# A graph network with an expert layer on one core: packed, gathered rows for 23 of the 49 aggregation tiles

## What is computed

```python
deg = segment_sum(ones, rows, n) + 1.0          # rows is src, cols is dst
dinv = rsqrt(deg)[:, None]
h = x @ W_in + b_in
for l in range(4):
    h_scaled = h * dinv
    msg = segment_sum(h_scaled[cols], rows, n) * dinv
    global_ctx = mean(h, axis=0) @ Wg[l] + bg[l]
    z = relu((h + msg) @ Wl[l] + bl[l] + global_ctx)
    h = (z - mean(z)) * rsqrt(var(z) + eps) * gamma[l] + beta[l]
```

## Time and profile before

| | |
|---|---|
| Median of 3 runs | 3345.32 us (3343.95 to 3345.57) |
| The profiled execution's span | 3340.5 us |
| TensorE, VectorE, ScalarE, GpSimd busy | 94%, 60%, 25%, 2% of the span |
| Setup, to about 45 us | 45 us |
| Counting, 45 to 597 us | 552 us |
| Flag, scales, table, 597 to 636 us | 39 us |
| Layers 1 to 4 | 573.6, 564.0, 563.4 and 614.0 us |
| Routing and experts, from 2951 us | 389.5 us |

### The profile page before, as it was taken

The page is one execution under the profiler, slowest core; times in us unless marked ns, Lnnn a source line. Parts: engine busy times, 40 slices in busy tenths (PEclk is TensorE's granted clock), DMA queues, the critical chain, the costliest instruction groups (busy, mean ns, idle before and its releaser), DMA issues.

```text
span 3340.5 us, 56169 instructions
## 1 busy us (share of the span) xinstructions
PE 3129.2 (94%) x17421; PEld 1810.2 (54%) x17421; DVE 1989.9 (60%) x5304; ACT 850.9 (25%) x1934; POOL 70.6 (2%) x168
## 2 busy tenths in 40 slices
PE   6888898699999999999999999999999999979998
PEld 4666676344444444444444444444444444458887
DVE  7999999755455445545554555455555555545554
ACT  3777787411111111111111111111111111123222
POOL 0000000000000000000000000000000000000100
PEclk8999999799999999999999999999999999989999
DMA  4222212412222222221222222221222222110000
GB/s 133 79 79 79 71 49 79 115 68 75 69 67 70 74 68 67 68 76 67 67 76 69 67 67 73 72 67 67 77 78 69 76 78 74 62 34 19 17 17 19
DMA packets 134136, 225.44 MB, mean 67 GB/s; under 512 B 12277, under 2 KB 106596, under 8 KB 134018
## 3 DMA queue, kind: packets, MB, share of 16 engines
q1 hardware_dynamic: 131666, 217.53, 20.2%
q0 software_dynamic: 2352, 6.40, 0.7%
HBM read 178.17 MB, written 45.74 MB: 67 GB/s over the span
## 4 chain that ended last, share of the span: by engine, by line
PE 80%; DVE 11%; issue 4%; ACT 2%; DVEq 1%; DMA 1%; SPq 0%; ACTq 0%; POOL 0%; POOLq 0%
PE bank L1342 50%; PE bank L1212 9%; PE bank L1416 5%; PE bank L1422 5%; PE bank L1300 4%; PE bank L1230 2%; PE bank L1198 2%; PE bank L1290 2%; PE bank L1228 1%; PE bank L1236 1%; DMA tab<-in_x 1%; DVE region L865 1%; DVE region L858 1%; DVE st L870 1%; DVE region L878 1%
## 5 line engine op out<-in xcount | busy, mean ns | idle before, releaser
L1342 PE MATMUL bank<-tab,region 128*128 128x512 f16 x9604 | 2143.0, 379 | 11.4 <-DMA region<-adjacency 11.2
L1342 PEld LDWEIGHTS bank<-tab,region 128*128 128x128 fp8e4 x9604 | 940.3, 98 | 1063.0 <-DVE tab L790 17.1
L1212 PE MATMUL bank<-region 128*128 128x320 bf16 x1862 | 316.4, 320 | 49.8 <-DVE region L670 48.3
L670 DVE TENSOR_SCALAR region<-iota_w,src_col,src_w 128x640 bf16<-128x640 int16 x931 | 361.0, 437 | 0.0
L865 DVE SCALAR_TENSOR_TENSOR region<-bank,c_back,bias 128x256 f32<-128x256 f32 x196 | 94.8, 483 | 405.7 <-PE bank L1300 405.7
L1029 ACT ACTIVATE tab<-region 128x640 fp8e4<-128x640 uint8 x490 | 307.2, 712 | 18.5 <-DVE region L701 18.5
L1212 PEld LDWEIGHTS bank<-region 128*128 128x128 f16 x1862 | 232.6, 144 | 124.4 <-DVE region L670 95.7
L1127 ACT ACTIVATE sd<-mv,eps_c 128x1 f32<-128x1 f32 x196 | 57.8, 295 | 820.8 <-DVE mv L872 820.8
L862 DVE TENSOR_TENSOR region<-bank,region 128x256 f16<-128x256 f32 x196 | 83.2, 425 | 297.6 <-ACT region L1125 297.6
L1125 ACT ACTIVATE region<-bank 128x256 f16<-128x256 f32 x196 | 75.3, 384 | 594.9 <-PE bank L1290 594.9
L1416 PE MATMUL bank<-tab 128*128 128x384 f32 (+1 forms) x544 | 177.2, 484 | 2.6 <-DMA b_s<-in_L_ffn_b 2.6
(11 more groups left out here) (194 smaller groups left out, 2143.9 us busy)
## 6 DMA issues: line engine op xcount, KB each, us to landing
region<-adjacency SPq DMA_DIRECT2D x196, 784.0 KB, 4.3
adjacency<-tab SPq DMA_DIRECT2D x12, 3136.0 KB, 13.9
region<-in_x POOLq DMA_DIRECT2D x48, 128.0 KB, 2.3
out<-region SPq DMA_DIRECT2D x48, 128.0 KB, 1.7
tab<-in_x SPq DMA_DIRECT2D x1, 6016.0 KB
tab<-in_L_ffn_W SPq DMA_DIRECT2D x4, 512.0 KB, 4.2
Wg_s<-in_L_gnn_Wg SPq DMA_DIRECT2D x1, 1024.0 KB
region<-in_L_gnn_Wl SPq DMA_DIRECT2D x1, 1024.0 KB, 5.6
```

Source lines behind the costliest of these rows:

```text
L670: ins = v.tensor_scalar(hot_s[:, j, :], iota_w[:], src_col[:, ds(start + j, 1)], src_w[:, ds(start + j, 1)], ALU.is_equal, ALU.mult)
L1212: ins = mm(bank[k % 2 * 2 + half][:, 0:HALF], hot_d[:, :, j], hot_s[:, j, half * HALF:(half + 1) * HALF], start=j == 0, stop=j == WIN - 1)
L1342: ins = mm(acc[a][:, :], A_s[:, a, m, :], tab[:, here + m, :], start=m == 0, stop=m == T - 1)
```

## The change

Of the 49 output tiles 23 are picked, the even ones from 2 to 46. An output tile has about 2041 edges, which reach some 1740 of the 6250 nodes. In layers 2 to 4 a picked tile's aggregation reads only rows that it needs, packed into 17 blocks (CAP) of 128: 17 matmuls stand where 49 stood. The packing keeps a node inside its group of 16 partitions, so each group has 17 x 16 = 272 places (TAKEN).

- **Counting.** VectorE compares each edge's source tile with the 23 picked tiles (two TENSOR_TENSORs a tile, 230 and 207 elements wide); the second matmul of each pair of L1212 gets 23 more columns. ScalarE takes the sign of the counts (23 columns a tile). Before the flag, VectorE sums these and makes a list of candidates (a code for each needed node), TensorE sums the groups, and the flag also turns on if a group has more than 272. SyncE writes the candidates to DRAM and loads them back in another shape, a row for each picked tile and group.
- **Layer 1.** All tiles are aggregated as before. VectorE picks the lists in 2 x 34 rounds of MAX8 and MATCH_REPLACE over 784 columns, three rounds in each of the first 24 tiles (behind L858, behind the split and behind the tile's last operation). ScalarE's queue writes the lists out and loads them back; then GpSimd fetches the picked rows of A by 17 indirect DMAs for each picked tile (from tile 14 and tile 26 on) and writes them out packed. SyncE waits for all of them before it starts any load of layer 2.
- **Layers 2 to 4.** ScalarE's queue writes each finished tile of the table to DRAM as well. At a layer's border GpSimd waits for all 49, then gathers: 17 indirect DMAs of 128 rows of 1 KB for each picked tile, in chunks of 6, 6 and 5, into four slots; a slot is used again once TensorE has read it. TensorE waits for each chunk. The load of A for a picked tile is 272 KB.
- **Order.** In a picked tile the turn and the product of the tile before stand ahead of matmuls 10 and 16, in the full tile behind a picked one ahead of matmuls 22 and 34. VectorE's order is unchanged: `late` is always false, so a tile's whole chain is completed before the sums of the next are taken. The layers' tiles are written out without loops on VectorE and ScalarE, and from layer 2 on on TensorE and SyncE, with constant indices. The reload of x in layer 4 moves from GpSimd's to ScalarE's queue. fgam and fbet are loaded at the end.

The core of the diff:

```diff
+PICKED = list(range(2, T - 2, 2))
+CAP = 17
+TAKEN = CAP * GROUP
+ROUNDS = TAKEN // 8
+PER_STEP = 3
+CHUNK = ((0, 6), (6, 12), (12, CAP))
+SLOTS = 4
+SPARSE_T, SPARSE_MM = 10, 16
+AFTER_T, AFTER_MM = 22, 34
+def late(l, t):
+    return False
...
+                for h in range(2):
+                    sp.wait_ge(pack_out[h], 16 * ((NS + 1 - h) // 2))
+                for l in range(1, LAYERS):
+                    for t in range(T):
+                        a = slot(t)
+                        sp.wait_ge(agg_done, l * T + t + 1)
+                        if picked(t):
+                            sp.dma_start(A32_s[:, a, 0:CAP * P // 4], AspD[PICKED.index(t)]).then_inc(a_in[a], 16)
+                        else:
+                            sp.dma_start(A32_s[:, a, :], A[t].rearrange("p m s -> p (m s)")).then_inc(a_in[a], 16)
...
+            def fetch_pack(q):
+                for j in range(CAP):
+                    nc.gpsimd.indirect_dma_start(pack[q % 2][:, j, :], None, A_rows,
+                                                 bass.IndirectOffsetOnAxis(ap=pick_A[:, q, j:j + 1], axis=0)
+                                                 ).then_inc(pack_in[q % 2], 16)
...
+            c = 0
+            for l in range(1, LAYERS):
+                hold(pool, rows_out[l - 1], 16 * T)
+                for q in range(NS):
+                    for j0, j1 in CHUNK:
+                        if c >= SLOTS:
+                            freed(c - SLOTS)
+                        for j in range(j0, j1):
+                            nc.gpsimd.indirect_dma_start(G[c % SLOTS][:, j - j0, :], None, tab_rows[(l - 1) % 2],
+                                                         bass.IndirectOffsetOnAxis(ap=pick_tab[:, q, j:j + 1], axis=0)
+                                                         ).then_inc(g_in[c % SLOTS], 16)
+                        c += 1
...
+                    v.tensor_tensor(hot_s[:, j0:j1, W:W + NS], pick_id[:, 0:NS].unsqueeze(1).to_broadcast([P, j1 - j0, NS]),
+                                    src_tile[:, ds(start + j0, j1 - j0)].unsqueeze(2).to_broadcast([P, j1 - j0, NS]),
+                                    ALU.is_equal)
...
+            def take(h, r):
+                top = lists[h][0:rows, 8 * r:8 * r + 8]
+                pick_own.done(v.max(top, left[h][0:rows, :]))
+                pick_own.wait()
+                ins = v.match_replace(left[h][0:rows, :], top, left[h][0:rows, :], 0.0)
...
+                for t in range(T):
+                    gathered(l, t)
+                    if l == 0:
+                        picking(t, 0)
+                    split(l, t)
+                    if l == 0:
+                        picking(t, 1)
+                    if not late(l, t):
+                        moments(l, t)
+                        normal(l, t)
+                    if l == 0:
+                        picking(t, 2)
...
+                a.activation(some[:, m, 0:NS], bank[k % 2 * 2 + 1][:, HALF:HALF + NS], ACT.Sign).then_inc(some_set, 1)
...
+                def picked_rows(l, t, c, turn_at, product_at):
+                    n, a, q = l * T + t, slot(t), PICKED.index(t)
+                    for h, (j0, j1) in enumerate(CHUNK):
+                        pe.wait_ge(g_in[(c + h) % SLOTS], 16 * g_count[(c + h) % SLOTS])
+                        for j in range(j0, j1):
+                            if j == turn_at:
+                                turn_u(n - 1)
+                            if j == product_at:
+                                product_u(n - 1, l)
+                            ins = mm(acc[a][:, :], A_s[:, a, j, :], G[(c + h) % SLOTS][:, j - j0, :], start=j == 0,
+                                     stop=j == CAP - 1)
```

More of the change, by code:

```diff
@@ L102, in build @@
     AG = nc.dram_tensor("adjacency_general", [FIELDS * PK, PLANES, P, T, P], BF16).ap()
+    candD = nc.dram_tensor("candidates", [NS, P, T], F32).ap()
+    listD = nc.dram_tensor("lists", [NS * GROUPS, TAKEN], F32).ap()
+    AspD = nc.dram_tensor("packed", [NS, P, CAP * P // 4], I32).ap()
+    TABD = [nc.dram_tensor(f"rows{h}", [P, T, 2 * D], F16).ap() for h in range(2)]
+    A_rows = A.rearrange("t p m s -> (t p m) s")
+    tab_rows = [TABD[h].rearrange("p t f -> (p t) f") for h in range(2)]
     ctx = ExitStack()
@@ L424, in read_flag, with slot @@
             return eng.value_load(flag[0:1, 0:1], min_val=0, max_val=1)
[L426 to L430, removed]
+        def slot(t):
+            return (t - 1) % RING if t else RING
         @block.sync
@@ new lines, in _, with picking, gathered @@
+            SPAN_B = -(-ROUNDS // PER_STEP)
+            def picking(t, part):
+                h, r = t // SPAN_B, t % SPAN_B * PER_STEP + part
+                if h < 2 and r < ROUNDS:
+                    take(h, r)
+                for h in range(2):
+                    if part == 0 and t == (h + 1) * SPAN_B + 2:
+                        chosen_rows(h)
+            def gathered(l, t):
+                n, a, here = l * T + t, slot(t), (l + 1) % 2 * T
+                tile_own.done(v.tensor_tensor(hs, tab[:, here + t, 0:D], tab[:, here + t, D:2 * D], ALU.add))
+                dve.wait_ge(lo_ready, n + 1)
+                tile_own.done(v.tensor_tensor(acc_s, acc[a][:, 0:D], lo_f[:, a, :], ALU.add))
+                tile_own.wait()
+                tile_own.done(v.tensor_scalar(Q, acc_s, c_read[:, t:t + 1], None, ALU.mult))
+                tile_own.wait()
+                v.scalar_tensor_tensor(out=U[:, 0, :], in0=hs, scalar=c_own[:, t:t + 1], in1=Q, op0=ALU.mult,
+                                       op1=ALU.add).then_inc(u_ready, 1)
@@ L844, in one @@
+            for l in range(LAYERS):
                 dve.wait_ge(ctx_done, l + 1)
@@ L909, in one @@
+                if l < LAYERS - 1:
                     dve.wait_ge(tab_ready, (l + 2) * T)
                     dve.sem_inc(hsum_ready, 1)
-            layers(dve, one)
             dve.wait_ge(xsum, T)
@@ L1133, in one @@
-                tiles(act, step, n0)
-            layers(act, one)
+                if l == LAYERS - 1:
+                    for t in range(RING):
+                        again(t)
+                for t in range(T):
+                    take_sums(l, t)
+                    if t and not late(l, t - 1):
+                        rows(l, t - 1)
+                    take_turned(l, t)
+                    if t and late(l, t - 1):
+                        deviation(l, t - 1)
+                        finish(l, t - 1)
+                    if not late(l, t):
+                        deviation(l, t)
+                        if t and late(l, t - 1):
+                            rows(l, t - 1)
+                        finish(l, t)
+                    if l == 0:
+                        for h in range(2):
+                            if t == (h + 1) * SPAN_B:
+                                lists_out(h)
+                            if t == (h + 1) * SPAN_B + 1:
+                                lists_in(h)
@@ L1137, in _ @@
+                rows(l, T - 1)
             act.wait_ge(xmean_done, 1)
@@ L1247, in _ @@
             ins.then_inc(norms_done, 1)
+            pe.wait_ge(taken_set, 1)
+            mm(bank[3][:, 0:NS], same_group, taken, start=True, stop=True).then_inc(taken_sum, 1)
             degrees(T - 1, 2 * MG)
```

373 lines of the change are left out of this document (267 added, 106 removed).

## The result

The changed kernel took 4103.8 us (4087.0 to 4132.7, 4 runs) against 3345.0 us before: a ratio of 1.2279, 95% interval 1.2229 to 1.2329. It is slower by 759 us. The later runs add something that no single comparison shows: **this kernel's time is not the same on every chip.** It took 3550.8 us on chip 5 and 3555.3 us (one execution) on chip 11, but 4162.3 us on chip 12, while the kernel before stayed within 3340 and 3357 us in every comparison. The chip of the first measurement is not on record; it may be chip 12 itself. So two things are to be explained: why the kernel is slower everywhere, and what costs 550 to 610 us more on one kind of chip.

A forecast was written before the change was run, and what follows sets the result against it. VectorE bounds counting, TensorE layers 1 to 3, one tile's serial chain layer 4. 3340.5 - 214 + 15 + 36 + 38 + 5 + 10 = 3230.5 us, forecast 3235 us; range 3185 to 3470 us.

The forecast's parts named there:

- Step 1: Layers 2 to 4: fewer matmuls, limited by the serial chain; 82, 82 and 50 us less, together -214 us.
- rival D: Layer 4: TensorE's clock falls at each of its 46 stalls, some 2 us lost in each, 3317 us; chance 0.05.
- step 6: Before the flag and layer 4: sums and candidates +5 us, row stores nothing, TensorE's clock +10 us (0 to 90).
- Step 2: Layers 2 to 4: GpSimd's gathers take 1.0 us per indirect DMA, hidden but for 7 us a layer at its start.
- rival A: GpSimd's queue: indirect issue takes 1.25 us or more, decides from about 1.16 us on; 3460 us, slower; chance 0.25.
- Step 3: Layer 1: 391 packing DMAs and 23 stores end at 1240 us, delaying layer 2's first load; +15 us.
- Step 4: Layer 1: VectorE's 68 picking rounds of 2.1 us make 24 tiles 13.0 us long against 11.45; +36 us.
- Steps 5 and 6: Counting: two more VectorE comparisons a tile, +38 us; then sums and candidates +5 us, clock in layer 4 +10 us.
- Rival C: GpSimd's issue: VectorE's three TENSOR_SCALARs a tile stop it for 11%, 1.0 becomes 1.11 us; 3278 us; chance 0.15.

The follow-up runs named there:

- experiment 7: Kernel before with GpSimd DMAs that nobody waits for added, another kind (indirect or direct) in each layer: 3342.0 and 3342.6 us against 3342.2 on chip 8.

## Why the prediction was wrong, point by point

- **Step 1, the chain: right in layers 2 and 3, wrong in layer 4.** The kernel without indirect DMAs shows what the step foresaw, TensorE's timeline in layer 2:

```profile
1515.03 0.44 PE L1553 MATMUL bank<-ident,region 128*128 128x128 f32 x2 [0.86 <-DVE region L1036]
...
1523.68 0.44 PE L1553 MATMUL bank<-ident,region 128*128 128x128 f32 x2 [1.29 <-DVE region L1036]
...
1533.62 0.44 PE L1553 MATMUL bank<-ident,region 128*128 128x128 f32 x2 [0.86 <-DVE region L1036]
```

  A pair takes 18.59 us (forecast 19.0), the stalls 0.86 and 1.29 us, ended by VectorE. The two layers gain 100 us each (forecast 82, of which 7 us were taken off for the start of the gathers, which this kernel lacks). In layer 4 the mechanism of **rival D**, given 0.05, is what happened:

```profile
2458.15 0.69 PE L1553 MATMUL bank<-ident,region 128*128 128x128 f32 x2 [2.48 <-DVE region L1036]
2458.64 4.20 PE L1642 MATMUL bank<-tab,region 128*128 128x512 f16 x12
2462.67 0.82 PE L1563 MATMUL bank<-Wx,region 128*128 128x256 f16 x6
...
2471.66 0.61 PE L1553 MATMUL bank<-ident,region 128*128 128x128 f32 x2 [2.78 <-DVE region L1036]
```

  After stalls of 2.5 to 3.2 us the transposes take 0.61 and 0.69 us as in the earlier trace rows, and twelve matmuls 4.20 instead of 2.6. Turn to product takes 4.52 us against 2.86, the granted clock of 2300 to 2750 us is 0.90 where the kernel before has 1.00 in its layer 4 (2400 to 2900 us). Layer 4 ends at 606.9 us against a forecast of 564: -6 instead of -50. The part of D that was wrong is its size: it does not fall at every stall (turn and product at 2483.89 to 2486.76 are fast), so it costs some 43 us, not 92, nor the 10 that step 6 had put down for the clock. Over the three layers the kernel without indirect DMAs gains 207 us where step 1 forecast 214; that the sums are so close is luck, since the errors of layers 2 and 3 and of layer 4 cancel. The chain itself was right: L1049 to L1036, 2463.53 to 2471.60, is 8.07 us (8.1).
- **Step 2, the gathers: the price was the error.** 0.97 us of work for each (forecast 1.0), but **another 0.30 us of issue time between two**, which was in neither of the terms that the step added up: the earlier trace rows hold direct DMAs issued one at a time, and direct ones back to back show no gap either (experiment 7). One in 1.25 us is past the 1.1 us at which the step said its cover ends. From the 3551 us execution:

```profile
1849.72 0.99 POOL L714 DMA_INDIRECT early<-rows,early  x1 [0.30 <-PE bank L1630]
1851.01 1.15 POOL L714 DMA_INDIRECT early<-rows,early  x1 [0.30 <-issue]
...
1852.46 0.94 POOL L714 DMA_INDIRECT early<-rows,early  x1 [0.30 <-PE bank L1630]
1854.01 1.89 PE L1630 MATMUL bank<-early,region 128*128 128x512 f16 x4 [1.75 <-DMA early<-rows,early]
```

  The packed tile waits in its third chunk, the sign named for rival A. Without the gathers layers 2 and 3 are 78 us shorter each. Turns at 1808.64 and 1894.02 span four pairs, 21.3 us each.
- **Step 3, the packing: +185 us, not +15** (layer 1 with it 772.3 us, without 587.1). It runs from 853.1 to 1418.9 us, 566 us where 408 were forecast: 98 from the rate, and the waits. Each buffer is wanted again right after its store is issued, so GpSimd waits for the landing (waits of the 3551 us execution: us in all, times, longest us):

```profile
POOL early L682 <- issue: 112.5, 369, 0.3
POOL early L714 <- DMA rows<-tab: 108.9, 3, 44.4
POOL early L714 <- PE bank L1630: 84.1, 50, 5.6
POOL early L682 <- DMA packed<-early: 61.9, 21, 6.5
```

  21 waits of 2.9 us, where the step had 0.2 us each.
- **Step 4, the picking:** rounds of 1.96 us (MAX8 966 ns, MATCH_REPLACE8 955, MATCH_VALUE_LOAD 88), forecast 2.1; about 20 of the 24 tiles at some 12.3 us, not 13.0; +13 us for the layer, not +36.
- **Steps 5 and 6:** the start of layer 1 moved by 31 to 35 us (forecast 43), the rest by 4 to 5.
- **Rival A** (0.25, 3460 us) is the case that came true on chips 5 and 11, 95 us short: the packing's store waits (+51 in layer 1), layer 4 (634 instead of 578, of which 43 are D's clock, which I had not joined to A), less 12 of setup. I had set its price and its sign rightly as a rival, and still took the value below it; its break-even of 1.16 us no run tested.
- **Rival C is small, and not as it was described.** In the 3551 us execution the gathers take 0.97 us in the mean against a median of 0.946, 2 to 3% more and not 11%; 204 of the 1564 indirect DMAs take over 1.0 us. The three TENSOR_SCALARs that C blamed are not what the long ones have in common: of 165 that ran beside an L1037, 43 took over 1.0 us, of 162 beside an L1055 3, of 156 beside an L1066 none, but of 169 beside an L947, which is no TENSOR_SCALAR, 109. VectorE pays too: L1037 takes 0.44 us in the mean beside an indirect DMA and 0.35 without, at times 0.56:

```profile
1839.38 1.08 POOL L714 DMA_INDIRECT early<-rows,early  x1 [0.30 <-issue]
...
1840.01 0.56 DVE L1037 TENSOR_SCALAR region<-region,c_read 128x256 f32<-128x256 f32 x1
```

  The Trainium skill (SBUF — State Buffer, "SBUF: two separate sides") has the lock on which C was built. These rows show that the two engines disturb each other; the counts above do not single out the operations that the prediction took to hold the lock, so they do not confirm it as the cause.
- **Not in the prediction at all:** that every other engine could be held up while GpSimd issues. It is 550 to 610 us of the 759 where it happens, more than every term of the sum, and it is what carries the result beyond the range and beyond rival A; without it step 2's price and step 3's waits alone make the change slower instead of faster. No view of the kernel before could show it, since that kernel has no indirect DMA. Its mechanism stays open.

## What to carry to other kernels

Price an operation that no row shows by its rhythm, not its duration: on chip 5 the kernel without indirect DMAs is 159 us faster than before, and the rate of one in 1.25 us, 0.30 us of it a gap, with the waits around it turns that into a loss of 206. Where a helper engine feeds the others, size its work to leave it slack: with every third tile instead of every second, the same code is 2.8% faster than before on a chip that issues indirect DMAs undisturbed. And measure a kernel with many indirect DMAs on several chips before you trust either number.

## What the runs showed of the hardware

- An indirect DMA on GpSimd has a nearly fixed price: 1.14 us with 16 rows, 1.25 us with 128, the same for 128-byte and 1 KB rows; a direct one 0.54 us.
- On chip 12 and on the chip of the first measurement (perhaps the same) a stage gets 0.58 to 1.05 us longer for each one, with the DMA engines 13% busy in 900 to 1000 us; the mechanism is open. On chips 5, 8, 11 and 15 391 to 1564 of them cost the others next to nothing but the wait for their data.
- TensorE's clock falls to its lower level after some stalls of 2.5 to 3.2 us and not after others; stalls of 0.9 to 1.3 us in layer 2 left the granted clock at 1.00 (1400 to 1600 us of the kernel without indirect DMAs).
